# Attention and low-rank FFN block: value bias folded into the output bias, values copied by ScalarE in four-tile groups, seed copies interleaved with exponentials

## The reference

```python
a = layernorm(x)
q = einsum('bsd,dhk->bshk', a, Wq) + bq ; k = ... Wk + bk ; v = ... Wv + bv
attn = softmax(einsum('bqhd,bkhd->bhqk', q / 8, k))
o = einsum('bhqk,bkhd->bqhd', attn, v)
x1 = x + layernorm(einsum('bqhd,hdm->bqm', o, Wo) + bo)
n = layernorm(x1)
out = x1 + layernorm(gelu(n @ U1 @ V1 + b1) @ U2 @ V2 + b2)
```

## Time and profile before

| | |
|---|---|
| median of 3 runs | 2403.34 us (2403.27 to 2405.83) |
| profiled execution, its own time | 2404.93 us |
| its span, first to last instruction | 2403.1 us |
| mean granted TensorE clock | 0.995 |
| TensorE busy (matmuls) | 2353.2 us (98%) |
| VectorE busy | 2040.7 us (85%) |
| ScalarE busy | 1398.1 us (58%) |
| GpSimd busy | 2109.0 us (88%) |

### The profile page before, as it was taken

The page is one execution under the profiler, slowest core; times in us unless marked ns, Lnnn a source line. Parts: engine busy times, 40 slices in busy tenths (PEclk is TensorE's granted clock), DMA queues, the critical chain, the costliest instruction groups (busy, mean ns, idle before and its releaser), DMA issues.

```text
span 2403.1 us, 43533 instructions
## 1 busy us (share of the span) xinstructions
PE 2353.2 (98%) x15628; PEld 1173.3 (49%) x15628; DVE 2040.7 (85%) x3264; ACT 1398.1 (58%) x1671; POOL 2109.0 (88%) x1206
## 2 busy tenths in 40 slices
PE   6999999999999999999999999999999999999998
PEld 3445454545445455444545444454544545444454
DVE  7888888888888888888888888888888888889877
ACT  5656556565555655656555555655556555655546
POOL 5888989888888888989888988988889888989986
PEclk9999999999999999999999999999999999999999
DMA  1000001000000000100001000100110100100101
GB/s 51 29 14 28 28 15 33 28 15 27 28 20 28 28 15 27 34 16 25 28 16 32 28 17 26 33 25 17 28 28 20 28 28 15 35 22 29 37 27 36
DMA packets 62969, 62.55 MB, mean 26 GB/s; under 512 B 28868, under 2 KB 46660, under 8 KB 62756
## 3 DMA queue, kind: packets, MB, share of 16 engines
q1 hardware_dynamic: 61748, 59.44, 8.4%
q10 hardware_dynamic: 1008, 0.33, 0.1%
HBM read 56.88 MB, written 2.61 MB: 25 GB/s over the span
## 4 chain that ended last, share of the span: by engine, by line
PE 87%; DVE 5%; ACT 3%; issue 2%; POOL 2%; DMA 0%; ACTq 0%; POOLq 0%; DVEq 0%
PE o_ps L443 34%; PE spare_ps L402 13%; PE score_ps L422 10%; PE score_ps L428 9%; PE score_ps L425 9%; PE spare_ps L388 3%; PE spare_ps L379 3%; PE spare_ps L488 3%; DVE max_part L866 2%; PE spare_ps L455 1%; PE spare_ps L370 1%; ACT probs L692 1%; POOL total L1141 1%; ACT score_ps L682 1%; DVE part_sum L902 1%
## 5 line engine op out<-in xcount | busy, mean ns | idle before, releaser
L1141 POOL TENSOR_TENSOR total<-total,probs 128x832 f32<-128x832 f32 (+1 forms) x896 | 1760.9, 1965 | 248.8 <-ACT probs L692 176.0
L866 DVE TENSOR_REDUCE max_part<-spare_ps 128x1 f32<-128x512 f32 x2027 | 1303.8, 685 | 273.2 <-PE spare_ps L402 256.4
L692 ACT ACTIVATE probs<-score_ps 128x1024 f32<-128x1024 f32 x1024 | 993.1, 1022 | 821.2 <-PE score_ps L428 820.6
L443 PE MATMUL o_ps<-probs,v_sb 128*64 128x512 f32 x4096 | 976.4, 597 | 0.0
L443 PEld LDWEIGHTS o_ps<-probs,v_sb 128*64 128x64 f32 x4096 | 271.9, 137 | 423.6 <-issue 289.5
L402 PE MATMUL spare_ps<-k_hi,q_hi 64*128 64x512 f32 x2027 | 462.0, 450 | 10.0 <-DVE max_part L866 6.5
L422 PE MATMUL score_ps<-q_hi,kd_hi 64*128 64x512 f32 x2048 | 413.5, 399 | 6.7 <-ACT score_ps L682 6.7
L428 PE MATMUL score_ps<-q_hi,kd_lo 64*128 64x512 f32 x2048 | 406.4, 391 | 0.0
L425 PE MATMUL score_ps<-q_lo,kd_hi 64*128 64x512 f32 x2048 | 404.9, 390 | 0.0
L402 PEld LDWEIGHTS spare_ps<-k_hi,q_hi 64*128 64x128 f32 x2027 | 194.4, 184 | 430.9 <-issue 241.8
L902 DVE TENSOR_REDUCE part_sum<-probs 128x192 f32<-128x768 f32 (+1 forms) x255 | 392.4, 1539 | 1.5 <-ACT probs L692 1.4
(11 more groups left out here) (137 smaller groups left out, 1105.8 us busy)
## 6 DMA issues: line engine op xcount, KB each, us to landing
m_all<-m_scratch SPq DMA_DIRECT2D x64, 512.0 KB, 4.4
denom<-denom_scratch SPq DMA_DIRECT2D x122, 128.0 KB, 3.0
m_scratch<-neg_rows SPq DMA_DIRECT2D x256, 1.0 KB
y_acc<-in_L_attn_x SPq DMA_DIRECT2D x8, 256.0 KB, 6.3
key_f<-in_L_attn_x SPq DMA_DIRECT2D x8, 256.0 KB, 2.9
block_out<-probs SPq DMA_DIRECT2D x8, 256.0 KB, 2.3
denom_col<-denom SPq DMA_DIRECT2D x61, 4.0 KB
denom_scratch<-denom_col SPq DMA_DIRECT2D x61, 4.0 KB, 1.4
```

Source lines behind the costliest of these rows:

```text
L443: last = nc.tensor.matmul(o_ps[half(h), :], v_sb[:, b, kt, half(h)], probs[:, st % RING, h, :], start=(kt == 0), stop=(kt == T - 1))
L692: nc.scalar.activation(probs[:, st % RING], score_ps[st % 2][:], ACT.Exp, scale=SCALE).then_inc(s["exp_done"], 1)
L866: nc.vector.reduce_max(max_part[:, G % 2, h, qt, kc:kc + 1], bank[max_bank(n, h)], AX.X).then_inc(s["max_done"], 1)
L1141: nc.gpsimd.tensor_tensor(others(total[:, G % 2], G), so_far, others(probs[:, st % RING], G), ALU.add).then_inc(s["sum_done"], 1)
```

## The change

- The value bias is taken out of the copy to `v_sb`. Instead, `bv` (as a column per head pair) and all of `Wo` are loaded at the start, GpSimd multiplies and sums them over the 8 head pairs (`pool_bias`, four instructions into the still unused `denom`), TensorE sums over partitions with `ones` (`Pe.bias`, in double 3), VectorE adds the result to `bo_sb` (`dve_bias`). The output's first use of `bo_sb` waits for that, and so does the first use of `denom`.
- The copy of values to `v_sb` goes from VectorE (`dve_v`) to ScalarE (`act_v`), four tiles at once: `V_AT` has four groups, all in `d` = 6, in place of eleven. The first unit's tables change accordingly.
- Two of the four key projections move from `d` = 7 to `d` = 0 of the next chunk (`K_AT`); the first unit's first key projections move up from double (1, 4) and (1, 7) to (1, 0) and (1, 4).
- At a boundary ScalarE's order is exponential, seed, exponential, seed, and keys or values behind them. Before it was exponential, exponential, keys, seed, seed.

```diff
-K_AT = {(0, 4): 0, (0, 7): 1, (1, 4): 2, (1, 7): 3}
-V_AT = {(0, 6): (0, 2), (1, 0): (2, 1), (1, 6): (3, 2), (2, 0): (5, 1), (2, 4): (6, 2), (2, 6): (8, 2), (2, 7): (10, 1),
-        (3, 0): (11, 1), (3, 4): (12, 1), (3, 6): (13, 2), (3, 7): (15, 1)}
+K_AT = {(0, 4): 0, (1, 0): 1, (1, 4): 2, (2, 0): 3}
+V_AT = {(0, 6): (0, 4), (1, 6): (4, 4), (2, 6): (8, 4), (3, 6): (12, 4)}
...
-FIRST_K_AT = {(1, 4): 0, (1, 7): 1, (2, 0): 2, (2, 4): 3}
-FIRST_V_AT = {(2, 7): (0, 4), (3, 0): (4, 4), (3, 4): (8, 4), (3, 7): (12, 4)}
+FIRST_K_AT = {(1, 0): 0, (1, 4): 1, (2, 0): 2, (2, 4): 3}
+FIRST_V_AT = {(1, 6): (0, 4), (2, 6): (4, 4), (3, 4): (8, 4), (3, 6): (12, 4)}
...
+            def bias(self):
+
+                self.pe.wait_ge(s["bias_scaled"], 4)
+                ps = self.take(SPARE["bias",], "bias", 0)
+                for k in range(2):
+                    last = nc.tensor.matmul(ps[half(k), 0:D], ones[:], bias_rows[:, 0, :], start=True, stop=True)
+                last.then_inc(s["bias_ps"], 1)
...
+        def act_v(act, u, t0, nt, name=None):
+            at = u * T + t0
+            act.wait_ge(s["v_ps"], at + nt)
+            if u >= 2 and t0 == 0:
+                act.wait_ge(s["pv_done"], (u - 1) * NC * T)
+            nc.scalar.activation(v_sb[:, u % B, t0:t0 + nt, :].rearrange("p t n -> p (t n)"), bank[name or SPARE["V", at]][:, 0:nt * P],
+                                 ACT.Copy).then_inc(s["v_done"], nt)
...
             act_k_high(act, 0, NC - 1)
             act_x(act, 4)
+            act_v(act, 0, 0, TC, FIRST_V_BANK)
             act_x(act, 5)
...
+                last = n + 1 < DOUBLES and d == PER_CHUNK - 1
                 act_exp(act, 2 * n)
+                if last:
+                    act_seed(act, 2 * n + 2)
                 act_exp(act, 2 * n + 1)
+                if last:
+                    act_seed(act, 2 * n + 3)
+                if values_at(u, c, d):
+                    act_v(act, *values_at(u, c, d))
                 if keys_at(u, c, d):
                     act_k(act, *keys_at(u, c, d))
...
-                if n + 1 < DOUBLES and d == PER_CHUNK - 1:
-                    act_seed(act, 2 * n + 2)
-                    act_seed(act, 2 * n + 3)
...
-            nc.vector.tensor_tensor(v_sb[:, u % B, t0:t0 + nt, :],
-                                    bank[name or SPARE["V", at]][:, 0:nt * P].rearrange("p (t n) -> p t n", t=nt),
-                                    b_v[:, u // B % 2, :].unsqueeze(1).to_broadcast([P, nt, P]), ALU.add).then_inc(s["v_done"], nt)
+        def dve_bias(dve):
+            dve.wait_ge(s["bo_in"], 16)
+            dve.wait_ge(s["bias_ps"], 1)
+            nc.vector.tensor_tensor(bo_sb[:], bank[SPARE["bias",]][:, 0:D], bo_sb[:], ALU.add).then_inc(s["bias_done"], 1)
...
+        def pool_bias(pool):
+
+            pool.wait_ge(s["bias_in"], 32)
+            nc.gpsimd.tensor_tensor(bias_rows, bias_rows, b_v[:].unsqueeze(2).to_broadcast([P, PAIRS, D]), ALU.mult).then_inc(s["bias_scaled"], 1)
+            for k, count in enumerate((4, 2, 1)):
+                pool.wait_ge(s["bias_scaled"], k + 1)
+                nc.gpsimd.tensor_tensor(bias_rows[:, 0:count, :], bias_rows[:, 0:count, :], bias_rows[:, count:2 * count, :],
+                                        ALU.add).then_inc(s["bias_scaled"], 1)
...
-                             (w_qkv[:, j, 2, :], wv_v[i]), (b_v[:, j, :], bv_v[i].partition_broadcast(P)),
+                             (w_qkv[:, j, 2, :], wv_v[i]),
...
+            sp.dma_start(bias_rows, wo_rows).then_inc(s["bias_in"], 16)
+            sp.dma_start(b_v[:], bv_v, allow_slow_non_contiguous=True).then_inc(s["bias_in"], 16)
             sp_m_out(sp, 0)
             sp_m_back(sp, 0)
```

More of the change, by code:

```diff
@@ L55 @@
 WO_AT = 1
+BIAS_AT = 3
 COLUMN_CHUNKS = 3
@@ L138, in spare_banks @@
             use("Wo", projected_at(G, d))
+        if n == BIAS_AT:
+            use("bias")
         if n in HEADS_AT:
@@ L171, in build @@
     bk_v = bk.rearrange("(i h) k -> i (h k)", h=2)
-    bv_v = bv.rearrange("(i h) k -> i (h k)", h=2)
+    bv_v = bv.rearrange("(i h) k -> (h k) i", h=2)
+    wo_rows = Wo.rearrange("(i h) k m -> (h k) i m", h=2)
     ctx = ExitStack()
@@ L187, in build @@
         b_qk = sb("b_qk", [P, 2, 2])
-        b_v = sb("b_v", [P, 2, P])
+        b_v = sb("b_v", [P, PAIRS])
         w_o = sb("w_o", [P, 2, D])
@@ L251, in build @@
             denom_copied col_dma recip_done scratch_dma recip_col_done y_half denom_dma o_copied o_norm_done wo_ps_ready y_done max_ready max_done
-            neg_max_done neg_rows_done""".split()
+            neg_max_done neg_rows_done bias_in bias_scaled bias_ps bias_done""".split()
         s = {n: ctx.enter_context(nc.semaphore(n)) for n in names}
@@ L256, in build @@
         m_dma = [s["m_dma0"], s["m_dma1"]]
-        W_DMA_N = 7 * 16
+        W_DMA_N = 6 * 16
         f_names = """v1_high v1_split f_low f_u1_ps f_u1 f_wst f_wmv f_wc f_ep1 f_nm1 f_ep2 f_ep3 ffn_w_in g_in0 g_in1 f_st1 f_mv1 f_rs1 f_t1 f_yn_late f_x1 f_x1_late f_st2 f_mv2
@@ L300, in half @@
             return slice(h * HD, (h + 1) * HD)
+        bias_rows = denom[:].rearrange("p h (i m) -> p (h i) m", m=D)
         FIRST_XT_BANK = ["o", "s10"] * 2 + ["o"] * 4
@@ L351, in take @@
                     pe.wait_ge(s["exp_done"], k + 1)
+                elif was == "bias":
+                    pe.wait_ge(s["bias_done"], 1)
                 elif was == "U":
@@ L590, in pe_program @@
                     me.head_projections(HEADS_AT[n])
+                if n == BIAS_AT:
+                    me.bias()
                 if n == CENTRE_AT:
@@ L941, in dve_y @@
             if G < B * NC:
-                dve.wait_ge(s["bo_in"], 16)
+                dve.wait_ge(s["bias_done"], 1)
                 dve.wait_ge(s["xn_done"], TC * (g + 1))
@@ L1052, in dve_program @@
                     dve_neg_max(dve, 0)
-                if n == T:
-                    dve_v(dve, 0, 0, TC, FIRST_V_BANK)
             for n in range(DOUBLES):
@@ L1073, in dve_program @@
                     dve_neg_max(dve, G + 1)
-                if values_at(u, c, d):
-                    dve_v(dve, *values_at(u, c, d))
+                if n == BIAS_AT:
+                    dve_bias(dve)
                 if projected_at(G, d) is not None:
@@ L1243, in pool_program @@
             first_rstd(7)
+            pool_bias(pool)
             for n in range(DOUBLES):
@@ L1315, in sp_denom_back @@
                 sp.wait_ge(s["o_norm_done"], G - 1)
+            elif G == 0:
+                sp.wait_ge(s["bias_ps"], 1)
             for h in range(2):
```

## The result

The changed kernel takes 2415.18 us in the median of 5 runs (2413.93 to 2417.22), the one before 2403.66 (2403.27 to 2407.13). The ratio is 1.0045, 95% interval 1.003 to 1.006: slower by some 11 us, where 2410.8 had been forecast, in a range of 2394 to 2421.

The account below looks back on a forecast made before the run. TensorE's queue was taken to bound the kernel, with ScalarE setting bare boundaries. Units 1 to 14 +8.3, unit 0 -0.5 and start -0.3 gave +7.5 us on 2403.3: 2410.8 us, range 2394 to 2421.

Parts of the forecast that it names:

- The seeds' new order: At chunk boundaries, seeds wait 0.03 us behind their exponentials: ScalarE's chain grows from 3.80 to 4.08 us, the boundary becomes 5.71.
- Rival 1: At boundaries, a wait for the own queue costs nothing: -0.28 for each of 60, 2394 us, deciding at 0.02 gap; 22%.
- rival 2: At boundaries, a seed's wait costs 0.14 us as on GpSimd: +0.22 each, +13 in all, 2424 us; 15%.
- Boundaries with keys: Two per unit, units 1 to 14: 5.71 us against 5.78 once the key projection's 0.91 moves out, -0.07 each.
- with a tile: Two boundaries per unit, units 1 to 14, lose their value tile: 5.71 us against 5.17, +0.54 each.
- Value projections: TensorE, units 1 to 14: four groups of four tiles take 3.70 us where eleven groups took 4.07, -0.35 per unit.
- VectorE's relief: VectorE loses 11 copies per unit, but TensorE waits for it only in double 6: no gain.
- ScalarE's copies: ScalarE gains four value copies in double 6, in idle time before the next exponential: no cost.
- Keys in double 0: ScalarE's exponentials and three key copies take under 4 us in the lengthened double 0: no cost.
- Unit 0: First unit: boundaries +0.28, -0.07 and +0.54 twice, a stall and key projections -1.8, together -0.5 us.
- Start: Kernel start: VectorE's shorter queue about -0.6 us, TensorE's bias matmuls +0.3, together -0.3 us.
- GpSimd's bias: Start: GpSimd's four bias instructions, near 5 us, lie in 13.5 us of its idle time.

Follow-up runs that it names:

- experiment 1: The changed kernel with ScalarE's old order at a boundary, both exponentials and then both seeds: 2398.2 us, ratio 0.9966 to the kernel before.
- experiments 6 and 7: The changed kernel with its four value groups in double 7 instead of 6, seeds interleaved (6) or both exponentials before both seeds (7): 2387.0 us each.
- experiment 5: The changed kernel with the old key and value tables and the old order on ScalarE: 2407.5 us, ratio 1.0002 to the kernel before.
- experiment 3: The kernel before with only the key tables of the changed kernel: 2401.0 us, ratio 0.9981 to the kernel before.

## Why the prediction was right, and where it was off

- **The seeds' new order** was the step on which the sign hung, and it held to the hundredth: a gap of 0.03 us (VectorE's, as taken), a chain of 4.08 us, a boundary of 5.71 us in every chunk. That the mechanism was right experiment 1 shows; it takes back 17 us, 60 times 0.28. That ScalarE's gap is the same as VectorE's was in part luck, for no row of before had one of ScalarE's. Rival 1 (such a wait is free) and rival 2 (GpSimd's 0.14) are out. Rival 1's break-even is misstated: by the prediction's own +7.5 us at a gap of 0.03 and 1.2 us for each 0.01, the sign turns at an overlap of 0.03, not at a gap of 0.02. The Trainium skill ("VectorE: DVE Perf Modes", section on the DRAIN) says of VectorE's copies that a semaphore after each adds nothing. Carried over to a wait on ScalarE this does not hold here: an exponential and the seed behind it overlap by 0.1 us where the seed waits for the exponential one earlier, and stand 0.03 apart where it waits for the one directly ahead.
- **Boundaries with keys, -0.07 each, and with a tile, +0.54 each**: with the chain as predicted and the lengths of before, they came out so. That cover can be put back, and what it is worth, experiments 6 and 7 show.
- **Value projections, -0.35 per unit: this step failed.** (The prediction's own figures, 4.07 less 3.70, make it -0.37.) There are four groups of 0.92 now, but the doubles that the others left pay the 0.05 in their value matmuls. Two of the seven groups lay in boundaries that ScalarE sets now, two in doubles that got the keys; three doubles became bare, 3 x 0.05 = 0.15 us per unit. With that the sum per unit is 0.59 + 0.15 = 0.74 against 0.76 measured in the mean, and 14 units give 10.4 of the 10.6 us. The trace of before had the two lengths of the value matmuls side by side; I read only the projections' own.
- **VectorE's relief, nothing; ScalarE's copies, nothing**: right in the steady state, by experiment 5.
- **Keys in double 0, nothing**: right in the change, but only because the value tile left that double; experiment 3 has the price of the two together.
- **Unit 0, -0.5 forecast, -0.9 measured**, with the stall gone.
- **Start, -0.3 forecast**, and -0.25 measured, but by luck. The first exponential starts anywhere from 47.2 to 49.2 us in the ten profiles, and in five kernels with all of this change's start from 47.2 to 48.5, so 0.3 us can't be told. The wait that VectorE's lighter queue was to shorten is as long as before:

```profile
45.63 0.79 PE L410 MATMUL spare_ps<-k_hi,q_hi 64*128 64x512 f32 x2 [1.60 <-DVE max_part L893]
```

- GpSimd's bias took 1.90 and 2.61 us in its idle time, where near 5 had been forecast:

```profile
36.70 1.90 POOL L1237 TENSOR_TENSOR denom<-denom,b_v 128x1024 f32<-128x1024 f32 x1
38.67 2.61 POOL L1240 TENSOR_TENSOR denom<-denom 128x512 f32<-128x512 f32 x3
```

- Unit 15 and the end are 0.8 us longer in the profiled execution. The prediction had nothing there, and no run was spent on it; it stays open. In the ten profiles this stretch takes from 198.7 to 202.2 us, so 0.8 may be scatter.

The forecast was 4.4 us short. On the profiled spans it is +7.5 against +10.3: units 1 to 14 are 2.3 us over the forecast, most of it the value projections, unit 15 with the end 0.8 over, unit 0 0.4 under. The other 1.6 us lie between the spans and the medians.

## What to carry to other kernels

Where an engine's chain lies under another engine's work, look at what else is under that cover before moving it away: the value tile in double 7 looked like load on the bound engine and was in fact free. (The keys there were not: ScalarE's copies of them stood ahead of the seeds, and their boundary was 0.35 us longer than their projection accounts for.) An instruction that waits for the one directly ahead of it on its own queue loses the overlap with it, here on ScalarE, so a consumer is better placed one instruction later than directly behind its producer, even if that makes the first result ready later; what counts is which wait ends last. And a group's fixed cost is only saved by merging groups if nobody else pays it when the group is gone.

## What the runs showed of the hardware

- On ScalarE, the waiting copy starts 0.03 us behind the end of its predecessor, in 125 of the 126 such places of the changed kernel, where independent neighbours overlap by 0.1 us (two exponentials in 1.94 us). The exponential behind a seed starts 0.07 before its end (1128.03 + 1.03 against 1128.99).
- After a wait for ScalarE, the first pair of score matmuls takes 0.33 us to the next group instead of 0.23 (1131.12 to 1131.45), so each such stall costs 0.1 us beyond its own length.
- The float32 value matmuls take 1.87 us directly behind the maximum matmuls and 1.82 behind another float32 projection.
- GpSimd's product of 1024 columns, one input broadcast, took 1.90 us, less than its sum of 832 columns at 1.97.
